# A four-layer graph network: long two-operand VectorE operations split or given a PSUM operand, and one small step of the last pass moved to GpSimd

## The chip, the cores and the metric

The kernel runs on one core of one Trainium2 chip. The metric is the device time of that core in microseconds, the median of the runs shown. Everything is float32 except the indices, which are int32.

## The reference

`x` is [50000, 256]; `src` and `dst` are 25000 edges sorted by `dst`. Four graph layers follow each other, each as `x = layernorm(x + layer(x))`:

```python
# layer 0: edges carry a product, nodes run an MLP with batch statistics
agg = segment_sum(x[dst] * edge_attr_256, src, N)
h1  = ((1 + eps) * x + agg) @ W1 + b1
out = relu(batchnorm(h1) * gamma + beta) @ W2 + b2
# layer 1: MLP over [x, mean of edge_attr_64 by src, u[0]]
out = relu(concat(x, agg64, u) @ W1 + b1) @ W2 + b2
# layer 2: attention over the edges of each dst, 8 heads of 32
e   = leaky_relu(a1[src] + a2[dst]); m = segment_max(e, dst)
ex  = exp(e - m[dst]); s = segment_sum(ex, dst)
out = elu(segment_sum(ft[src] * ex / s[dst], dst))
# layer 3: the same with 4 heads of 64, self loops, and out = elu(out + bias) + x
```

## The kernel before, in words

The program is seven stages, with a barrier of all engines after each (`barrier`). The rows of `x` go in steps of 512 (4 rows to each of 128 partitions, `J = 4`); that is 98 steps over the nodes (`NS`) and 49 over the edges (`ES`, `CS`). Each engine runs its own program in order; the order is written out by hand and kept by semaphore waits (`wait`, `wait_ge`). SyncE (SP) issues the large transfers, GpSimd (POOL) the indirect ones, one instruction for each 128 rows.

- **Stage 1** (`p1_*`), edges of layers 0 and 1. Before the steps SP fills a table `tab0` with zeros. POOL gathers `x[dst]` (L397, four per step) and scatter-adds the sums (L408, four per step). VectorE compares the step's source indices (L440), counts earlier equal ones with a masked reduction against the constant `early` (L446) and multiplies the gathered rows by `edge_attr_256` (L456, 1024 columns). TensorE adds rows of one source, ScalarE copies them out.
- **Stage 2** (`p2_*`) and **stage 3** (`p3_*`) are layer 0's batch statistics and the two MLPs. The change does not touch them.
- **Stage 4** is `edge_pass(2)`. POOL gathers the source rows of step s+3 (L1068) and scatters the finished rows of step s-1 (L1079), alternately, four of each per step. TensorE transposes and projects them; VectorE runs the running sum along each partition's edges: the products with the new weights (L1252), four times a multiply and an add of 256 columns (L1263, L1267), and a division over all 1024 columns (L1276). The scatters of a step wait for that one division.
- **Stage 5** is `node_pass`, elu, residual, layer norm and the projection for layer 3. ScalarE makes relu and exp (L1413, L1415), VectorE the elu (L1484) and the residual (L1487), both 1024 columns with two SBUF operands, statistics (L1493, L1497), the normalisation's shift (L1478) and the copy-out of the projection (L1471). ScalarE normalises (L1423) once the shift is there, and only behind that does it make the exp of the step after next. POOL computes the power (L1448) and scatters four narrow pieces per step (L1454).
- **Stage 6** is `edge_pass(3)`. It has no matmuls in its steps; L1256 multiplies 1024 gathered columns, then L1263 and L1267 run as in stage 4, and each scatter waits for its L1267.
- **Stage 7** is `last_pass`. POOL multiplies two blocks of 1024 columns (L1647, twice per step, back to back), adds the epsilon (L1653) and takes the power (L1656). TensorE adds the two blocks in PSUM (L1598), ScalarE makes relu and exp and the normalisation (L1624), VectorE the elu (L1712), the residual (L1716), `shift` (L1704: minus mean times the power's result, 4 columns, issued after L1716 of the next step), statistics (L1722, L1726) and, in even and odd steps, `factors` or `shares` (L1676 to L1697, 32 or 64 columns). SP loads three blocks and stores one per step, 2.1 MB together.

## Time and profile before

| | us |
|---|---|
| median of 3 runs | 5930.69 |
| the runs | 5925.17 to 5933.20 |
| the profiled execution, its own time | 5937.27 |
| the profiled execution, its span | 5935.2 |

The profile is of one execution; spans of single instructions come from it. "Idle before" names what ended an engine's idle time in front of a group. The busy share of the transfer engines ("DMA share") and the rate in GB/s stand in the view of the stretches. Engines are named PE (TensorE), PEld (its weight loads), DVE (VectorE), ACT (ScalarE), POOL (GpSimd) and SP (SyncE).

### The profile page before, as it was taken

To read this page: it belongs to the slowest core of one execution; us is meant where nothing else is said; L and a number is where in the kernel's file an instruction comes from. 1 tells how busy PE (TensorE), PEld (TensorE's weight loads), DVE (VectorE), ACT (ScalarE), POOL (GpSimd) and SP (SyncE) were. 2 spreads that over 40 slices of the span, in tenths; PEclk is the share of its full clock that TensorE was granted. 3 is DMA by queue.
4 is the path that set the end of the run, shared out by engine and by line. 5 is a ranking of instruction groups with operands and counts; after the bars stand their busy time and mean duration, and the time that the engine had idled before them with its cause. 6 is when DMAs were issued, how large, how long until landed. Compare 5 with 4: busy or idle time off the path is not lost. (4 is left out here: it accounts for less than half of the span.)

```text
span 5935.2 us, 70230 instructions
## 1 busy us (share of the span) xinstructions
PE 4263.1 (72%) x16758; PEld 2808.8 (47%) x16758; DVE 3817.1 (64%) x9802; ACT 1982.9 (33%) x3296; POOL 3712.2 (63%) x3263
## 2 busy tenths in 40 slices
PE   0566639989999999999999877756777500036665
PEld 0344415546666666666666567655555300012222
DVE  1344435656666666666666567767887655569998
ACT  0111105542222222222222222226777400026666
POOL 2378854445555555555555577766888777767776
PEclk6778869999999999999999988879999855568888
DMA  9987769983333333333333244438999633369997
GB/s 358 380 175 138 140 112 363 366 297 122 120 117 117 117 117 117 117 117 117 117 117 117 72 140 134 132 106 292 308 306 304 211 93 91 92 209 331 320 322 265
DMA packets 497940, 1125.24 MB, mean 190 GB/s; under 512 B 165814, under 2 KB 248714, under 8 KB 497814
## 3 DMA queue, kind: packets, MB, share of 16 engines
q1 hardware_dynamic: 346380, 913.22, 45.0%
q0 software_dynamic: 113184, 174.84, 12.4%
q10 hardware_dynamic: 38250, 35.85, 2.0%
q8 instruction: 36, 0.59, 0.0%
q14 instruction: 90, 0.74, 0.0%
HBM read 623.20 MB, written 543.83 MB: 197 GB/s over the span
## 5 line engine op out<-in xcount | busy, mean ns | idle before, releaser
L942 PE MATMUL psum<-arena,W1b 128*128 128x512 f32 x1568 | 725.3, 605 | 0.0
L965 PE MATMUL psum<-W2b,arena 128*128 128x256 f32 x3136 | 725.2, 379 | 0.0
L730 DVE TENSOR_SCALAR arena<-arena 128x256 f32<-128x256 f32 x784 | 462.4, 651 | 302.2 <-POOL arena L725 300.0
L536 PE MATMUL psum<-arena 128*128 128x324 f32 x980 | 362.9, 538 | 372.6 <-DVE arena L456 254.1
L1598 PE MATMUL psum<-arena,ident 128*128 128x512 f32 x784 | 433.5, 706 | 240.9 <-POOL arena L1647 240.9
L965 PEld LDWEIGHTS psum<-W2b,arena 128*128 128x128 f32 x3136 | 573.1, 190 | 66.3 <-issue 0.5
L855 ACT ACTIVATE arena<-psum,hbias 128x512 f32<-128x512 f32 x392 | 269.3, 687 | 860.2 <-PE psum L942 860.2
L1404 PE MATMUL psum<-Wg,arena 128*128 128x264 f32 x1568 | 396.6, 409 | 175.5 <-ACT arena L1429 175.5
L1454 POOL DMA_INDIRECT ad_d<-arena,FE x392 | 450.9, 1150 | 113.0 <-issue 111.2
L1079 POOL DMA_INDIRECT tab<-arena,IDX x392 | 412.7, 1053 | 122.9 <-issue 93.4
L721 POOL TENSOR_TENSOR arena<-arena,lneps 128x4 f32<-128x4 f32 x196 | 39.1, 200 | 713.9 <-DVE arena L717 711.3
L942 PEld LDWEIGHTS psum<-arena,W1b 128*128 128x128 f32 x1568 | 281.7, 189 | 429.9 <-issue 429.9
L819 POOL DMA_INDIRECT xd_d<-arena,FE x392 | 412.0, 1051 | 106.2 <-issue 105.9
L536 PEld LDWEIGHTS psum<-arena 128*128 128x128 f32 x980 | 229.8, 240 | 490.0 <-issue 379.5
L1404 PEld LDWEIGHTS psum<-Wg,arena 128*128 128x128 f32 x1568 | 304.5, 199 | 250.2 <-ACT arena L1429 198.8
L408 POOL DMA_INDIRECT tab<-arena x196 | 325.6, 1661 | 144.7 <-issue 54.6
L1598 PEld LDWEIGHTS psum<-arena,ident 128*128 128x128 f32 x784 | 168.2, 225 | 505.5 <-issue 482.8
L1138 PE MATMUL psum<-ident,arena 128*128 128x128 f32 x24 | 5.8, 433 | 543.9 <-DVE arena L1293 532.3
L1647 POOL TENSOR_TENSOR arena<-arena 128x1024 f32<-128x1024 f32 x196 | 368.9, 1903 | 18.0 <-DVE arena L1697 18.0
L918 PE MATMUL psum<-W2a,arena 128*128 128x256 f32 x1568 | 356.1, 380 | 23.0 <-ACT arena L841 23.0
L683 PE MATMUL psum<-arena,W1a 128*128 128x512 f32 x784 | 353.9, 594 | 0.0
L633 POOL DMA_INDIRECT fe_d<-EID,FIRST x196 | 200.0, 1021 | 242.9 <-ACT arena L658 198.3
(220 smaller groups left out, 9283.2 us busy)
## 6 DMA issues: line engine op xcount, KB each, us to landing
arena<-tab SPq DMA_DIRECT2D x194, 544.0 KB
arena<-in_x SPq DMA_DIRECT2D x194, 512.0 KB, 4.5
x_d<-arena SPq DMA_DIRECT2D x194, 512.0 KB, 3.6
arena<-x_d SPq DMA_DIRECT2D x194, 512.0 KB, 7.1
tab<-zero SPq DMA_DIRECT2D x132, 486.0 KB, 11.7
tab<-blank SPq DMA_DIRECT2D x97, 544.0 KB
h_d<-arena SPq DMA_DIRECT2D x97, 528.0 KB, 4.9
arena<-h_d SPq DMA_DIRECT2D x97, 528.0 KB, 5.6
```

Source lines behind the costliest of these rows:

```text
L536: last = pe.matmul(psum[:, 2 + j, 0:TW0], same[:, k.slot(2), i, j * P:(j + 1) * P], msg[:, k.slot(NX), i, :], start=(i == j), stop=(i == J ...
L683: last = pe.matmul(psum[:, 4 + 2 * b + g, :], W1a[:, f, g * P:(g + 1) * P], hT[:, b, f, :], start=(f == 0), stop=(f == FH - 1))
L730: v.tensor_scalar(y[:, j, :], r[:, j, :], self.mv[:, j, 0:1], self.rs[:, j:j + 1], ALU.subtract, ALU.mult).then_inc(self.s["y"], 1)
L819: pool.indirect_dma_start(out=xd_d[:, :], out_offset=bass.IndirectOffsetOnAxis(ap=FE[:, s * J + j:s * J + j + 1], axis=0), in_=x2[:, s % 2 ...
L918: last = pe.matmul(outA(j), p3y[:, f, j * P:(j + 1) * P], W2a[:, f, :], start=(f == 0), stop=(f == FH - 1))
L942: last = pe.matmul(psum[:, BR + c % RING, :], W1b[:, f, c * P:(c + 1) * P], x1T[:, f, :], start=False, stop=(f == FH - 1))
L965: last = pe.matmul(outB(j), hid[:, c, j * P:(j + 1) * P], W2b[:, c, :], start=(c == 0), stop=(c == KH - 1))
L1079: pool.indirect_dma_start(out=tab[:, :], out_offset=bass.IndirectOffsetOnAxis(ap=IDX[:, 2, c:c + 1], axis=0), in_=fin[:, s % NG, j, :], in ...
L1404: last = pe.matmul(psum[:, 2 + j, 0:HW], xT[:, f, j * P:(j + 1) * P], Wg[3][:, f, :], start=(f == 0), stop=(f == FH - 1))
L1454: pool.indirect_dma_start(out=ad_d[:, :], out_offset=bass.IndirectOffsetOnAxis(ap=FE[:, c:c + 1], axis=0), in_=hs[:, k.slot(NB), j, D + H3 ...
L1598: last = pe.matmul(psum[:, b + i, :], ident[:, :], a[:, k.slot(2), 2 * i:2 * i + 2, :].rearrange("p j d -> p (j d)"), start=(n == 0), stop ...
L1647: pool.tensor_tensor(out=a[:, b, :, :].rearrange("p j (h c) -> p j h c", h=H), in0=t[:, k.slot(NB), :, 0:D].rearrange("p j (h c) -> p j h ...
```

## The change

It touches five stages.

- Stage 1: `early` is copied once to PSUM bank 6, and the masked reduction reads it there. L456 becomes four multiplies of 256 columns. `hbias`'s matmuls move from bank 6 to bank 2.
- Stage 4: the maximum and the reciprocal of the sums are made before the running sum instead of behind it; L1276 becomes four divisions of 256 columns (`divided`), the one for row j issued after the add of row j+1; each scatter waits for its own division. The wait for the old scatter of the row buffer stands ahead of the running sum.
- Stage 5: the elu is written to PSUM in two operations of 512 columns; the residual reads it from there.
- Stage 6: the weights of a step are also written to PSUM, by a second exp on ScalarE (`near`), and the products of L1256 (`tB`) lie in PSUM; L1256, L1263 and L1267 then have one SBUF operand each.
- Stage 7: `shift` is gone from VectorE. VectorE makes minus the mean (`neg`, 4 columns) behind the step's statistics, after a wait for them, and GpSimd multiplies it by the power's result.

```diff
 # stage 1, VectorE
+            v.tensor_copy(psum[:, 6, :], early[:, :]).then_inc(s_c["id"], 1)
...
-                    v.tensor_tensor_reduce(out=junk[j], in0=same[:, b, j, 0:(j + 1) * P], in1=early[:, (J - 1 - j) * P:J * P], scale=1.0, scalar=0.0,
+                    v.tensor_tensor_reduce(out=junk[j], in0=same[:, b, j, 0:(j + 1) * P], in1=psum[:, 6, (J - 1 - j) * P:J * P], scale=1.0, scalar=0.0,
...
-                v.tensor_tensor(out=msg[:, k.slot(NX), :, 0:D], in0=xg[:, k.slot(NX), :, :], in1=eat[:, k.slot(NX), :, :], op=ALU.mult).then_inc(q["msg"], 1)
+                for j in range(J):
+                    v.tensor_tensor(out=msg[:, k.slot(NX), j, 0:D], in0=xg[:, k.slot(NX), j, :], in1=eat[:, k.slot(NX), j, :], op=ALU.mult).then_inc(q["msg"], 1)
 # stages 4 and 6, GpSimd's scatter
                     if L == 3:
                         pool.wait_ge(r["S"], J * s + j + 1)
-                    elif j == 0:
-                        pool.wait_ge(r["full"], s + 1)
+                    else:
+                        pool.wait_ge(r["full"], J * s + j + 1)
 # stages 4 and 6, ScalarE and VectorE
+                    if L == 3:
+                        act.activation(near(s), dd, ACT.Exp).then_inc(r["near"], 1)
...
+            tB = take([J, D]) if L == 2 else psum[:, 0:2, :].rearrange("p a (j d) -> p (a j) d", d=D)
...
+                    w1p, w2p = (w1[:, :, 1:J + 1], w2[:, :, 1:J + 1]) if L == 2 else (near(s)[:, 0, :, :], near(s)[:, 1, :, :])
...
+                    if L == 2:
+                        v.wait_ge(r["s"], s + 1)
+                        wait(v, r["full"], J * s)
+                        v.tensor_scalar(inv, sums[:, :, cur], 1e-30, None, ALU.max).then_inc(r["inv"], 1)
+                        v.wait_ge(r["inv"], 2 * s + 1)
+                        v.reciprocal(inv, inv).then_inc(r["inv"], 1)
+                    wait(v, sc[c], 16 * J * (s // NG))
...
+                        if L == 2 and j > 0:
+                            divided(s, j - 1)
+                    if L == 2:
+                        divided(s, J - 1)
+                def divided(s, j):
+                    if j == 0:
+                        v.wait_ge(r["inv"], 2 * s + 2)
+                    v.wait_ge(r["S"], J * s + j + 1)
+                    v.tensor_tensor(out=fin[:, s % NG, j, 0:D].rearrange("p (h c) -> p h c", h=H), in0=row[:, s % NG, j, 0:D].rearrange("p (h c) -> p h c", h=H),
+                                    in1=heads(inv[:, :, j]), op=ALU.mult).then_inc(r["full"], 1)
 # stage 5, VectorE
+                    for i in range(2):
+                        v.scalar_tensor_tensor(out=unit[:, 2 * i:2 * i + 2, :], in0=ex[:, b, 2 * i:2 * i + 2, :], scalar=-1.0,
+                                               in1=tt[:, k.slot(NB), 2 * i:2 * i + 2, 0:D], op0=ALU.add, op1=ALU.max).then_inc(r["elu"], 1)
...
-                    v.tensor_tensor(out=rr[:, b, :, :], in0=xt[:, k.slot(NB), :, :], in1=rr[:, b, :, :], op=ALU.add).then_inc(r["r"], 1)
+                    v.tensor_tensor(out=rr[:, b, :, :], in0=xt[:, k.slot(NB), :, :], in1=unit, op=ALU.add).then_inc(r["r"], 1)
 # stage 7, GpSimd's rstd, then VectorE
+                    pool.wait_ge(r["rs"], k.s + Z + 1)
+                    pool.wait_ge(r["neg"], k.s + 1)
+                    pool.tensor_tensor(out=nm[:, b, :], in0=neg[:, b, :], in1=rsd[:, b, :], op=ALU.mult).then_inc(r["nm"], 1)
...
-                    if not (k.known() and k.s == 0):
-                        shift(k.plus(-1))
...
+                    v.wait_ge(r["mv"], J * (k.s + Z + 1))
+                    wait(v, r["nm"], k.s + Z - 1)
+                    v.tensor_scalar(neg[:, b, :], mv[:, b, :, 0], -1.0, None, ALU.mult).then_inc(r["neg"], 1)
```

## Rows read from the trace of the kernel before

**Rows 1.** The page: span and instructions.

```profile
span 5935.2 us, 70230 instructions
```

**Rows 2.** Stretches of stages 4, 5, 6, 7: length, busy (instructions) by engine, clock, DMA share, GB/s.

```profile
3411.00:3994.00 583.00, 419.69 (x2408) 377.82 (x2408) 410.42 (x1346) 140.48 (x297) 430.69 (x395) 0.84 0.40 126
3996.00:4712.00 716.00, 501.07 (x2352) 390.27 (x2352) 556.58 (x1372) 496.81 (x784) 552.74 (x489) 0.95 0.91 294
4716.00:5253.00 537.00, 6.74 (x28) 5.99 (x28) 303.83 (x1049) 25.30 (x101) 404.74 (x394) 0.50 0.30 91
5256.00:5935.00 679.00, 433.52 (x784) 168.21 (x784) 601.29 (x1617) 408.37 (x637) 484.28 (x392) 0.86 0.90 309
```

**Rows 3.** GpSimd's transfer lines: ns (minimum/median/maximum), first and last start.

```profile
L397 POOL DMA_INDIRECT arena<-in_x,arena x196: 942/947/1850, 12.0 to 781.5; - x196
L408 POOL DMA_INDIRECT tab<-arena x196: 1552/1578/2385, 230.6 to 859.5; - x196
...
L1068 POOL DMA_INDIRECT arena<-x_d,IDX x196: 941/976/1934, 3417.6 to 3948.4; - x196
```

**Rows 4.** Groups by shape over the whole span: busy us, mean ns, idle before.

```profile
L408 POOL DMA_INDIRECT tab<-arena x196 | 325.6, 1661 | 144.7 <-issue 54.6 <-DMA tab<-zero 52.8 <-DMA tab<-arena 21.7
...
L397 POOL DMA_INDIRECT arena<-in_x,arena x196 | 195.8, 999 | 189.3 <-DVE arena L456 123.9 <-issue 52.1 <-DMA arena<-in_dst 6.2
```

**Rows 5.** Groups by shape inside stage 4, 3435 to 3985 us.

```profile
L1079 POOL DMA_INDIRECT tab<-arena,IDX x196 | 214.5, 1094 | 63.2 <-issue 61.1 <-PE psum L1113 1.5 <-ACT arena L1166 0.3
L1068 POOL DMA_INDIRECT arena<-x_d,IDX x184 | 201.4, 1095 | 64.9 <-issue 46.9 <-ACT arena L1156 12.9 <-ACT arena L1166 2.9
```

**Rows 6.** Timeline of one step of stage 4: start us, duration us.

```profile
3703.55 1.22 DVE L1276 TENSOR_TENSOR arena<-arena 128x1024 f32<-128x1024 f32 x1
3703.76 1.86 POOL L1068 DMA_INDIRECT arena<-x_d,IDX  x1 [0.30 <-issue]
```

**Rows 7.** Groups by shape inside stage 6, 4760 to 5230 us.

```profile
L1068 POOL DMA_INDIRECT arena<-h_d,IDX x176 | 184.3, 1047 | 53.7 <-issue 53.7
L1079 POOL DMA_INDIRECT tab<-arena,IDX x177 | 178.3, 1007 | 53.9 <-issue 28.3 <-DVE arena L1267 25.6
```

**Rows 8.** Timeline of one step of stage 5, DVE and ACT.

```profile
4301.34 1.23 DVE L1484 SCALAR_TENSOR_TENSOR arena<-arena 128x1024 f32<-128x1024 f32 x1 [0.78 <-ACT arena L1415]
...
4304.11 2.07 ACT L1423 ACTIVATE arena<-arena 128x256 f32<-128x256 f32 x4 [1.83 <-DVE arena L1478]
...
4308.26 1.23 DVE L1484 SCALAR_TENSOR_TENSOR arena<-arena 128x1024 f32<-128x1024 f32 x1 [0.60 <-ACT arena L1415]
```

**Rows 9.** Timeline of stage 4: two half-width operations with a PSUM operand, merged.

```profile
3709.72 1.26 DVE L1252 TENSOR_TENSOR arena<-psum,arena 128x512 f32<-128x512 f32 x2
```

**Rows 10.** VectorE lines of stages 7 and 3: minimum/median/maximum ns, first and last start.

```profile
L1712 DVE SCALAR_TENSOR_TENSOR psum<-arena,psum x98: 1205/1222/1230, 5281.4 to 5922.8; 128x1024 f32<-128x1024 f32 x98
L873 DVE TENSOR_SCALAR arena<-arena x98: 153/155/1905, 1325.9 to 3347.6; 128x4 f32<-128x4 f32 x98
```

**Rows 11.** Groups by shape inside stage 7, 5281 to 5923 us.

```profile
L1704 DVE SCALAR_TENSOR_TENSOR arena<-arena 128x4 f32<-128x4 f32 x96 | 113.7, 1185 | 0.0
...
L1653 POOL TENSOR_TENSOR arena<-arena,lneps 128x4 f32<-128x4 f32 x97 | 19.3, 199 | 151.8 <-DVE arena L1726 151.1
```

**Rows 12.** Timeline of one step of stage 7 in which L1704 did not wait.

```profile
5404.28 1.22 DVE L1712 SCALAR_TENSOR_TENSOR psum<-arena,psum 128x1024 f32<-128x1024 f32 x1
...
5404.89 3.77 POOL L1647 TENSOR_TENSOR arena<-arena 128x1024 f32<-128x1024 f32 x2
...
5409.84 1.23 DVE L1712 SCALAR_TENSOR_TENSOR psum<-arena,psum 128x1024 f32<-128x1024 f32 x1 [0.17 <-issue]
5410.01 3.77 POOL L1647 TENSOR_TENSOR arena<-arena 128x1024 f32<-128x1024 f32 x2
```

**Rows 13.** Transfers of stage 7 from 5300 to 5900 us.

```profile
DMA packets 51768, 192.82 MB, mean 321 GB/s; under 512 B 5764, under 2 KB 5764, under 8 KB 51767
```

**Rows 14.** Transfers of stage 2 from 900 to 1300 us.

```profile
DMA packets 79576, 142.71 MB, mean 357 GB/s; under 512 B 10349, under 2 KB 56250, under 8 KB 79569
```

70 lines of the change are left out of this document (30 added, 40 removed).

## The prediction

> **What bounds the kernel now.** I read the stretches first [rows 2], because a busy share over the whole span mixes stages with different limits. Then, for each stage that the change touches, I asked which engine never waits. The reader should see four answers.
>
> *Stages 1, 4 and 6* are held by GpSimd's queue of indirect transfers. In stage 4, 380 of them take 415.9 us busy [rows 5], and behind nearly each stands 0.30 us that waits for nothing the trace shows [rows 6], 114 us: 530 of that window's 550. In stage 6 it is 362.6 us busy and 353 times 0.30, 469 of 470 [rows 7]. In stage 1, from the first scatter at 230.6 us to the last at 859.5 [rows 3], the scatters take 325.6 us, the 168 gathers in that time 168 us, and the gaps 109 us: 603 of 629 [rows 4]. VectorE is busy for only 410 of 583 us and 304 of 537 [rows 2], so its own length is not the price there. What costs is how long GpSimd's instruction takes: a gather has a median of 0.976 us and a maximum of 1.934 [rows 3], and the long one starts 0.21 us into the 1024-column L1276 and takes 1.86 us [rows 6]. It does its 0.9 us of work after L1276 has ended.
>
> *Stage 5* looks the same but isn't. ScalarE waits 1.83 us per step for VectorE's shift; from the elu's start to that wait's end are 2.77 us, from there to the next elu's start 4.15 us, and the step is the sum, 6.92 us [rows 8]. It is a ring of ScalarE and VectorE; GpSimd runs beside it.
>
> *Stage 7* is held by VectorE: 98 starts of L1712 from 5281.4 to 5922.8 us are 6.61 us apart [rows 10], GpSimd waits 151 us for the statistics, and the shift on four columns takes 1.185 us on average [rows 11]. A 4-column operation needs 0.155 us when nothing is in its way [rows 10]; the rest is waiting while L1647 runs. In a step in which it didn't wait, L1712 to L1712 is 5.56 us, and GpSimd's period is 5.12 [rows 12]. Transfers run at 90% busy [rows 2].
>
> **The change, part by part.** The sum is made against the profiled execution, 5937.3 us (span 5935.2 [rows 1]); the median shown, 5930.7, is 6.6 lower, and I carry the difference over to it.
>
> *Stage 1.* Gathers average 0.999 us against a median of 0.947, scatters 1.661 against 1.578 [rows 3, 4]: 196 times 0.052 and 0.083 is 26 us over the median, the most that can be got. The masked reduction no longer has two SBUF operands; the multiply still has, in pieces that can hold GpSimd a third as long. I take two thirds, **-18 us**; the ends are -26 and 0. The split costs VectorE three more fixed parts, about 0.155 each, what an operation on 4 columns takes [rows 10], 0.5 us a step, hidden under the queue. The copy to PSUM and the moved bank cost nothing: the fill of the table covers them until 230 us.
>
> *Stage 4.* The excess is 196 times (1.095 - 0.976) for gathers and 196 times (1.094 - 1.007) for scatters, the base of the latter from stage 6's mean: 40 us [rows 3, 5, 7]. One L1276 per step takes 0.88 us of it [rows 6] when it meets a start; 49 would be 43. The divisions in quarters stay two-SBUF operations of the kind of L1267, and stage 6, full of those, has 0.07 us excess on gathers and none on scatters [rows 3, 7]. I take **-25 us**; ends -40 and 0. VectorE gets the same 0.5 us a step longer, and has 3.5 idle [rows 2]. The earlier wait for the old scatter concerns one issued before the gathers this step waited for. VectorE's step would be some 9.0 us, under the queue's 10.8 (530 us over 49). Next late would be ScalarE's copy, already 12.9 us [rows 5].
>
> *Stage 5.* Blocked scatters get shorter, but lie beside the ring: 0. On the ring the elu becomes two halves. Two 512-column operations with a PSUM operand take 1.26 us together [rows 9] against 1.23 [rows 8]; I add one wait's slack and take 0.05 us for 98 steps, **+5 us**. Ends: 0, and 0.2 a step, +20.
>
> *Stage 6.* The three products leave the two-SBUF kind altogether. Gathers average 1.047 against 0.976; 196 times 0.07 is 14, **-13 us**, ends -14 and 0. The second exp of ScalarE (a few tenths of a us) and its wait stand where VectorE has 4.7 us idle per step [rows 2]; were that cover gone, 49 times 0.3 would be 15 us.
>
> *Stage 7.* VectorE loses the shift, 1.185 us a step, and gains the negation, 0.155 [rows 10], and the wait for the statistics, about 0.1 (no row shows it; between 0 and 0.2): 6.61 - 1.185 + 0.255 is 5.68 us. GpSimd gains an operation of L1653's size, 0.2 us [rows 11], and its wait, 0.14: 5.12 + 0.34 is 5.46 [rows 12]. Behind this wait stand L1647's two products, but both sides of it start from the same statistics, so it ends early. Then transfers are next: 192.8 MB in 600 us is 2.13 MB a step of 6.61 us [rows 10, 13]; at stage 2's 357 GB/s [rows 14] that takes 5.97. The three lie so close that the slowest plus a little jitter holds: 6.0 us. 97 times (6.61 - 6.0) is **-59 us**. Ends: 5.7 a step, -88; 6.35, -25.
>
> The rows on which the negation hangs: L873, also a scalar operation on 4 columns, takes 0.155 us by median and once 1.905 [rows 10], so it can be held too. The Trainium skill, "SBUF — State Buffer", section Who interferes with whom, says that a `tensor_scalar` in a two-port mode and a GpSimd instruction fully block each other; the trace agrees, and by that alone the negation would be no better placed than the shift. I don't take it so, because GpSimd is idle, waiting for these very statistics, when they end: 151 us of waiting in 97 steps [rows 11].
>
> Sum: -18 - 25 + 5 - 13 - 59 = -110 us. 5930.7 - 110 is **5821 us**.
>
> **The rivals.** *The transfer queues aren't eased (12%).* The long gathers would come from something else than the two-SBUF kind. For it: no row shows what a long transfer of stage 1 lies beside. Against it: [rows 6]. Then stages 1, 4 and 6 give 0, 5931 - 54 = 5877. A rule of the Trainium skill, same page and section, points that way: it infers that `tensor_tensor` does not stall descriptor generation, which needs the write interface. The row with 1.86 us speaks against it.
>
> *Transfers hold stage 7 near today's rate (13%).* They are 90% busy already; 6.35 us a step gives -25 there and 5855 in all.
>
> *Stage 7 runs at VectorE's 5.7 us (6%).* 5792.
>
> *The negation waits like the shift did (6%).* Then stage 7 is 6.61 + 0.1 a step, +10; 5931 - 51 + 10 = 5890.
>
> *Slower (3%).* The two L1647 stand back to back for 3.77 us [rows 12]. If the negation fell behind both in every step, VectorE's step would be 5.5 + 3.77 = 9.3 us, stage 7 +260, the whole 6140. It decides from a mean wait of 1.5 us on: then the step is 7.14, which eats the 51 us of the other stages. Against it: GpSimd idle at that point.
>
> **How the numbers follow.** The forecast has 60%. The range 5785 to 5882 takes in the forecast with its bounds and the first three rivals, and leaves out the last two and the far ends. A measurement of this kernel tells about 0.2%, 12 us, from no change. All cases but the last are faster by more; I leave 3% for same because several small terms could fall out together: 0.94, 0.03, 0.03.
>
> **What would show it.** Stage 4: no transfer of GpSimd near 1.9 us, means near 1.02; the stage some 558 us. Stage 6: gathers all near 0.98, the stage 524. Stage 5: the step 6.92 to 7.0, scatters shorter, GpSimd waiting more. Stage 7: L1712 about 6.0 us apart, transfers at 350 GB/s, the negation at 0.15 to 0.3 us. I am wrong if the negation averages over 1 us, if the 0.30 us gaps grow, or if stage 5 moves by more than 20 us.

## The result, and the profile after

The changed kernel takes **5887.75 us** (median of 4 runs, 5881.5 to 5894.84) against 5931.67 for the kernel before (4 runs): a ratio of 0.9925, 95% interval 0.9913 to 0.9937. The forecast was 5821 us with a range of 5785 to 5882, so it was faster, as said, but by 44 us in place of 110, and the time lies above the range. The ratios of this document leave out two executions far outside the rest (8714 us in run e13, 8141 in run e15).

The page of the changed kernel, its span:

```profile
span 5892.9 us, 71391 instructions
```

Its stretches of stages 4, 5, 6 and 7, with columns as in [rows 2]:

```profile
3397.00:3963.00 566.00, 421.52 (x2408) 379.08 (x2408) 406.52 (x1493) 140.43 (x297) 411.19 (x395) 0.83 0.41 130
3965.00:4695.00 730.00, 512.93 (x2352) 400.06 (x2352) 562.87 (x1470) 497.81 (x784) 502.52 (x490) 0.93 0.89 288
4697.00:5222.00 525.00, 6.73 (x28) 5.98 (x28) 300.84 (x1049) 29.67 (x150) 391.30 (x395) 0.50 0.31 93
5224.00:5892.00 668.00, 419.40 (x784) 164.56 (x784) 550.61 (x1617) 403.63 (x637) 505.20 (x490) 0.87 0.90 314
```

Windows are cut by hand and a few us off. For sums I use the time from GpSimd's drain at one stage's end to the next, in the profiled execution of each kernel. That is one execution of each; the changed kernel's is the slowest of its four (5894.84 us), so that single terms are good to some us and no better:

```
stage (us)         1      2       3      4      5      6      7
kernel before    863.3  447.1  2100.1  584.6  718.7  541.1  673.1
changed kernel   848.4  447.2  2100.2  568.3  732.1  526.6  663.8
difference       -14.9   +0.1    +0.1  -16.3  +13.4  -14.5   -9.3
forecast           -18      -       -    -25     +5    -13    -59
```

Two terms come within some 3 us of the forecast, two miss it by 8 or 9. The fifth, stage 7, is short by 50.

The groups of GpSimd's transfers in stages 1, 4 and 6 of the changed kernel (us busy, mean ns, idle before), which answer to [rows 4, 5, 7]. L409, L398, L1088 and L1077 are the L408, L397, L1079 and L1068 of before:

```profile
L409 POOL DMA_INDIRECT tab<-arena x195 | 311.5, 1597 | 95.4 <-issue 54.3 <-DMA tab<-arena 22.3 <-DVE arena L456 18.3
L398 POOL DMA_INDIRECT arena<-in_x,arena x164 | 159.8, 974 | 50.0 <-issue 42.7 <-DVE arena L456 6.7 <-ACT arena L358 0.6
...
L1088 POOL DMA_INDIRECT tab<-arena,IDX x196 | 208.4, 1063 | 63.3 <-issue 53.0 <-ACT arena L1165 4.3 <-DVE arena L1298 2.4
L1077 POOL DMA_INDIRECT arena<-x_d,IDX x196 | 200.0, 1021 | 69.1 <-issue 43.0 <-ACT arena L1165 16.2 <-ACT arena L1177 6.2
...
L1088 POOL DMA_INDIRECT tab<-arena,IDX x196 | 197.2, 1006 | 59.7 <-issue 37.5 <-DVE arena L1287 22.2
L1077 POOL DMA_INDIRECT arena<-h_d,IDX x196 | 191.1, 975 | 59.8 <-issue 58.6 <-DVE arena L1287 0.9 <-ACT arena L1177 0.3
```

The first pair is stage 1, the second stage 4, the third stage 6. In stage 6 the gathers went from 1047 to 975 ns. In stage 4 both kinds are shorter, but not at the 976 and 1007 ns that I took for unhindered. Counted over stage 4, 33 transfers took over 1.5 us before and none does now.

Groups of stage 7 (VectorE and GpSimd) of the changed kernel. L1735 and L1739 are the elu and the residual (before L1712 and L1716), L1750 is the new negation, L1704 to L1712 are `factors`, and L1678 is before's L1653 [rows 11]:

```profile
L1735 DVE SCALAR_TENSOR_TENSOR psum<-arena,psum 128x1024 f32<-128x1024 f32 x98 | 120.0, 1224 | 24.7 <-ACT arena L1642 21.9 <-issue 2.5
L1739 DVE SCALAR_TENSOR_TENSOR arena<-arena,psum 128x1024 f32<-128x1024 f32 x98 | 119.6, 1221 | 23.3 <-ACT arena L1649 15.5 <-DVE psum L1735 6.3
...
L1706 DVE SCALAR_TENSOR_TENSOR arena<-arena 128x32 f32<-128x32 f32 x49 | 22.9, 468 | 1.7
L1708 DVE TENSOR_TENSOR arena<-arena 128x32 f32<-128x32 f32 x49 | 20.9, 427 | 1.7
...
L1750 DVE TENSOR_SCALAR arena<-arena 128x4 f32<-128x4 f32 x98 | 16.6, 170 | 3.4
L1711 DVE TENSOR_TENSOR arena<-arena 128x32 f32<-128x32 f32 x49 | 14.5, 295 | 1.7
L1704 DVE TENSOR_TENSOR arena<-arena 128x32 f32<-128x32 f32 x49 | 14.4, 293 | 39.1 <-DMA arena<-tab 36.1 <-issue 2.6
L1712 DVE TENSOR_TENSOR arena<-arena 128x32 f32<-128x32 f32 x49 | 12.5, 255 | 0.0
...
L1678 POOL TENSOR_TENSOR arena<-arena,lneps 128x4 f32<-128x4 f32 x98 | 19.7, 201 | 118.5 <-DVE arena L1747 115.1
```

The negation takes 170 ns: the part of the forecast that concerned the moved step came true, and the 1.0 us for which the shift was held each step is gone. Three things stand in its place. The five lines of `factors` sum to 85.2 us, where in the run with GpSimd's wait below the same five take 50.3. VectorE waits 36 us for table rows, 19 of them before the stage's first step, as in every run. And it waits 21.9 and 15.5 us for ScalarE. The kernel before had the second in small: its first line of `factors` waited 23.5 us, the same 19 at the start and 4 later.

```profile
L1676 DVE TENSOR_TENSOR arena<-arena 128x32 f32<-128x32 f32 x49 | 10.1, 206 | 23.6 <-DMA arena<-tab 23.5
```

The first two can be seen in one step of the changed kernel's timeline (start us, duration us):

```profile
5409.51 0.17 DVE L1750 TENSOR_SCALAR arena<-arena 128x4 f32<-128x4 f32 x1
...
5411.20 0.19 DVE L1704 TENSOR_TENSOR arena<-arena 128x32 f32<-128x32 f32 x1 [1.53 <-DMA arena<-tab]
5411.25 3.77 POOL L1672 TENSOR_TENSOR arena<-arena 128x1024 f32<-128x1024 f32 x2
5411.43 1.78 DVE L1706 SCALAR_TENSOR_TENSOR arena<-arena 128x32 f32<-128x32 f32 x1
5413.24 1.83 DVE L1708 TENSOR_TENSOR arena<-arena 128x32 f32<-128x32 f32 x1
5415.10 0.19 DVE L1711 TENSOR_TENSOR arena<-arena 128x32 f32<-128x32 f32 x1
...
5415.31 1.22 DVE L1735 SCALAR_TENSOR_TENSOR psum<-arena,psum 128x1024 f32<-128x1024 f32 x1
```

The table row of the step lands 1.5 us late, so `factors` starts together with GpSimd's two products (L1672), and two operations on 32 columns wait for one whole product each. From L1735 at 5404.84 to this one the step takes 10.5 us. The ten longest steps of the stage all have this form: a wait of 0.9 to 1.5 us for the table, then two operations of 1.8 to 1.9 us. Of the 97 steps 40 are under 5.8 us, as forecast for VectorE alone, and 10 are over 8.5; the mean is 6.51. Before it was 6.61 with 59 steps between 6.2 and 7. The loss is no longer spread evenly. It sits in a few long steps.

### The profile page after: what moved, and what is told of

It reads as the page before. It is cut to its first block and busy times, and to the rows that moved or that the text cites. A ratio compares the mean times of both kernels' runs of the same rounds, so it can differ in the third digit from the quotient of the medians.

```text
span 5892.9 us, 71391 instructions
## 1 busy us (share of the span) xinstructions
PE 4264.3 (72%) x16758; PEld 2816.8 (48%) x16758; DVE 3772.7 (64%) x10195; ACT 1984.3 (34%) x3345; POOL 3632.6 (62%) x3361
## 5 line engine op out<-in xcount | busy, mean ns | idle before, releaser
L1623 PE MATMUL psum<-arena,ident 128*128 128x512 f32 x784 | 419.4, 687 | 243.9 <-POOL arena L1672 235.8
L1426 PE MATMUL psum<-Wg,arena 128*128 128x264 f32 x1568 | 409.9, 419 | 169.9 <-ACT arena L1451 169.9
L1088 POOL DMA_INDIRECT tab<-arena,IDX x392 | 405.6, 1035 | 123.1 <-issue 90.5
L1476 POOL DMA_INDIRECT ad_d<-arena,FE x392 | 400.7, 1022 | 113.3 <-issue 113.0
L409 POOL DMA_INDIRECT tab<-arena x196 | 313.1, 1597 | 147.3 <-issue 54.3
L1672 POOL TENSOR_TENSOR arena<-arena 128x1024 f32<-128x1024 f32 x196 | 369.3, 1906 | 18.0 <-DVE arena L1725 15.5
```

What stands on the lines that cost most here:

```text
L1088: pool.indirect_dma_start(out=tab[:, :], out_offset=bass.IndirectOffsetOnAxis(ap=IDX[:, 2, c:c + 1], axis=0), in_=fin[:, s % NG, j, :], in ...
L1426: last = pe.matmul(psum[:, 2 + j, 0:HW], xT[:, f, j * P:(j + 1) * P], Wg[3][:, f, :], start=(f == 0), stop=(f == FH - 1))
L1476: pool.indirect_dma_start(out=ad_d[:, :], out_offset=bass.IndirectOffsetOnAxis(ap=FE[:, c:c + 1], axis=0), in_=hs[:, k.slot(NB), j, D + H3 ...
L1623: last = pe.matmul(psum[:, b + i, :], ident[:, :], a[:, k.slot(2), 2 * i:2 * i + 2, :].rearrange("p j d -> p (j d)"), start=(n == 0), stop ...
L1672: pool.tensor_tensor(out=a[:, b, :, :].rearrange("p j (h c) -> p j h c", h=H), in0=t[:, k.slot(NB), :, 0:D].rearrange("p j (h c) -> p j h ...
```

## The experiments

All but the runs whose edit says otherwise start from the changed kernel. The runs fell on five chips. On those of the first four and the last three runs the kernel before takes 5936 and 5938 us. On the other three chips (eleven runs) it takes 6027, 6034 and 6029 us, and so much of the difference lies in stages 4 and 6 that every run there has to be read stage by stage. Each chip was used at one time only, so "chip" below may also stand for something else that differed between those times. Durations as above:

```
stage (us)                        1      4      5      6      7
first four runs
e1  stage 5 as before           848.5  566.2  718.3  526.2  653.8
e2  GpSimd's wait               848.4  567.3  732.3  526.2  644.2
e3  six table slots             848.8  566.0  730.9  526.3  659.0
e4  fewer bytes                 850.0  566.7  731.0  526.3  618.0
other chips
e5  e1 + e2                     848.6  631.8  718.0  599.3  643.0
e6  e1 + e2 + e3                850.6  634.0  719.2  593.8  626.1
e7  only stage 7 changed        860.2  630.7  718.3  582.4  665.5
e8  three splits undone         859.9  630.7  723.5  591.7  678.6
e9  e2 + e4                     849.4  643.2  732.7  602.2  614.9
e10 before, fewer bytes         862.1  643.6  717.5  583.9  664.7
e11 division whole              847.5  637.9  730.6  599.5  657.0
e12 as e6                       848.7  640.5  721.0  596.9  623.2
e13 changed kernel              851.1  633.2  732.5  600.6  661.9
e14 as e11                      851.6  633.3  732.8  598.4  657.8
e15 as e6                       849.7  631.4  719.0  595.2  627.5
last three runs
e16 empty waits in stage 6      851.5  568.2  732.2  526.4  658.0
e17 stage 6 as before           850.7  565.9  730.9  541.3  665.6
e18 e6 with fewer waits         851.4  563.0  718.5  526.2  660.5
```

The changed kernel's own stage 7 spreads from 654 to 666 us over the profiles in which it is unaltered (e8 has 679). So less than some 12 us in stage 7 of one profile says nothing, and e8 shows that even 25 can occur.

### Stage 5 as it was

```diff
-                    for i in range(2):
-                        v.scalar_tensor_tensor(out=unit[:, 2 * i:2 * i + 2, :], ...)
+                    v.scalar_tensor_tensor(out=rr[:, b, :, :], in0=ex[:, b, :, :], ...)
...
-                    v.tensor_tensor(out=rr[:, b, :, :], in0=xt[:, k.slot(NB), :, :], in1=unit, ...)
+                    v.tensor_tensor(out=rr[:, b, :, :], in0=xt[:, k.slot(NB), :, :], in1=rr[:, b, :, :], ...)
```

> The changed kernel with stage 5 as it was before. Stage 5 took 13.5 us more after the change (732.2 against 718.7 us between the drains) while its scatters got shorter. Theory: GpSimd was beside the ring of ScalarE and VectorE, so undoing the edit gives the 13 us back: about 5874 us. Rival: the stages disturb each other, and the loss stays: 5887.

Ratio 0.9913 (0.9895 to 0.9931), and stage 5 is back at 718.3 us: its edit costs 13.8. By median the whole is only 7 us shorter (5880.87), within what stage 7 varies; the run doesn't decide between 5874 and 5887 for the whole, but stage 5 itself came back, here and at 718.0 in e5. Groups of VectorE in stage 5, first the changed kernel, then this run:

```profile
L1506 DVE SCALAR_TENSOR_TENSOR psum<-arena 128x512 f32<-128x512 f32 x196 | 127.4, 695 | 78.7 <-ACT arena L1437 78.7
L1493 DVE TENSOR_TENSOR arena<-psum,bias 128x1056 f32<-128x1056 f32 x98 | 123.3, 1258 | 64.4 <-PE psum L1426 62.4 <-issue 0.3
L1511 DVE TENSOR_TENSOR arena<-arena,psum 128x1024 f32<-128x1024 f32 x98 | 119.6, 1221 | 11.2 <-DVE psum L1506 9.4
```

```profile
L1493 DVE TENSOR_TENSOR arena<-psum,bias 128x1056 f32<-128x1056 f32 x98 | 123.3, 1258 | 56.7 <-PE psum L1426 56.6
L1509 DVE TENSOR_TENSOR arena<-arena 128x1024 f32<-128x1024 f32 x98 | 120.1, 1225 | 7.6
L1506 DVE SCALAR_TENSOR_TENSOR arena<-arena 128x1024 f32<-128x1024 f32 x98 | 120.0, 1224 | 79.7 <-ACT arena L1437 79.7
```

The halves hold VectorE 7.4 us longer (127.4 against 120.0), the residual waits 3.6 more, and the copy-out of the projection 7.7 more for TensorE, whose granted clock is 0.93 in place of 0.95. That is 18.7 us of the ring, somewhat more than the stage lost. Whether the clock is a cause of the longer wait for TensorE or goes along with the longer step isn't shown.

### GpSimd waits for the factors

```diff
                     rstd(k)
+                    if k.slot(2) == 0 and live(k.plus(4), NS):
+                        pool.wait_ge(r["d"], 2 * (k.plus(4).turn(2) + 1))
                     if live(k.plus(3), NS):
                         shared(k.plus(3))
```

> The changed kernel, in stage 7 GpSimd's products of an even step wait until VectorE has made that step's factors. Theory A (late table, then blocked factors): 12 of the 97 steps take 10.2 to 10.5 us, because the factors start late, behind a transfer, and two of their small operations then each wait for a whole 1.9 us product. With the guard these steps take 7 to 8 us, and the kernel 25 to 35 us less, about 5857. Rival B (the transfers' rate holds the stage): the waits only move, same time within 8 us. Rival C (GpSimd is the bound): GpSimd now waits longer, 10 to 20 us slower.

Ratio 0.989 (0.9873 to 0.9907). Stage 7 takes 644.2 us, 19.6 less, and no step is over 8.5 us. The whole is 17 us shorter by median, less than the 25 to 35 that I expected. In e5 the stage comes out at 643.0 again. Its groups of VectorE:

```profile
L1708 DVE SCALAR_TENSOR_TENSOR arena<-arena 128x32 f32<-128x32 f32 x49 | 11.2, 228 | 1.7
L1706 DVE TENSOR_TENSOR arena<-arena 128x32 f32<-128x32 f32 x49 | 11.0, 224 | 65.7 <-DMA arena<-tab 64.4 <-issue 1.2
```

The factors are no longer held, but VectorE now waits 64 us for the table rows in place of 36 (46 in place of 17 behind the first step). Part of what the wait saves goes into this.

### Six slots for the table rows

```diff
-            tt = take([NB, J, TW])
-            ht = take([NB, J, HW])
+            NQ, PER = 6, 12
+            tt = take([NQ, J, TW])
+            ht = take([NQ, J, HW])
...
-                    if live(k.plus(NB + 3), NS):
-                        tables(k.plus(NB + 3))
+                    if live(k.plus(NB + 5), NS):
+                        tables(k.plus(NB + 5))
```

> The changed kernel, in stage 7 the blocks of the table and of h have six slots instead of four and are loaded two steps earlier. Theory A: the factors never wait for a transfer, so they don't fall behind the products; the steps of 10 us go, stage 7 from 664 to 605-620 us, the kernel about 5835. Rival B (the rate of the transfers holds the stage): the queue is only longer, stage 7 stays within 15 us of 664. Rival D (TensorE at its lower clock and ScalarE hold it): the long steps go, but the others stay at 6.3 on average, stage 7 about 640.

Ratio 0.9904 (0.9887 to 0.992), stage 7 at 659 us. VectorE's groups:

```profile
L1739 DVE SCALAR_TENSOR_TENSOR psum<-arena,psum 128x1024 f32<-128x1024 f32 x98 | 120.1, 1225 | 66.5 <-ACT arena L1646 41.7 <-issue 24.6
...
L1708 DVE TENSOR_TENSOR arena<-arena 128x32 f32<-128x32 f32 x49 | 11.2, 229 | 23.2 <-DMA arena<-tab 18.6 <-issue 2.9
```

The wait for the table rows is gone but for the first two (18.6 us in all), and so is the holding of `factors`; the elu (here L1739) idles 66.5 us instead, 24.6 of them with no releaser. That last part isn't a wait of the schedule. Five steps take 11.6 to 12.2 us, and each is the first behind a jump of VectorE's loop: `run_beats` writes `PER` steps into the loop's body, 12 here in place of 4, and the five are steps 24, 36, 48, 60 and 72, counted from 0. One such step, VectorE alone, and below it the same place in e15, which also has six slots:

```profile
5395.44 0.23 DVE L1729 TENSOR_TENSOR arena<-arena 128x64 f32<-128x64 f32 x1
5401.71 1.23 DVE L1739 SCALAR_TENSOR_TENSOR psum<-arena,psum 128x1024 f32<-128x1024 f32 x1 [6.05 <-issue]
```

```profile
5516.34 0.23 DVE L1729 TENSOR_TENSOR arena<-arena 128x64 f32<-128x64 f32 x1
5516.87 1.23 DVE L1739 SCALAR_TENSOR_TENSOR psum<-arena,psum 128x1024 f32<-128x1024 f32 x1 [0.30 <-issue]
```

The trace has the branch itself in e3 at 5395.54 us and VectorE's next instruction, a register operation of the loop, at 5401.60. The five jumps of e3 take 5.7 to 6.4 us. In every other run but e18 no jump of VectorE takes over 0.28 us, in any stage. Counted from when the elu had all it waits for, the five cost 27 us. Without them stage 7 would be near 632 us (an estimate, 659 less 27), close to the 626 of e6: the six slots by themselves bring some 30 us, and the slow jumps take them back here. By its total this run looked like the rival in which the transfers' rate holds the stage, and it isn't: e6, e12 and e15 move the same bytes at 332 to 335 GB/s, against 314 in the changed kernel (e12's stretch of stage 7):

```profile
5356.00:5982.00 626.00, 417.77 (x784) 162.83 (x784) 516.59 (x1617) 403.11 (x637) 504.22 (x490) 0.88 0.94 335
```

### Fewer bytes in stage 7

The x rows are loaded for 16 of 128 partitions from the fifth step on, so part of the final sum is computed from old rows.

```diff
+                    if not (k.known() and k.s < NB):
+                        a, n = a[0:16], 16
                     sp.dma_start(xt[0:n, b, :, :], a).then_inc(n_x[b], 16)
```

> The changed kernel, in stage 7 the rows of x come from HBM for 16 of the 128 partitions only, from the fifth step on (what is computed from the other rows is not the reference's). A quarter of the stage's bytes is gone, nothing else. Theory A: tables land in time, stage 7 600 to 620 us. Rival B: the rate was the bound, stage 7 falls by up to a quarter until VectorE's 5.6 us a step holds, 560 to 580. Rival D: 640 or more.

Stage 7 falls to 618 us, 46 less, in the stretch

```profile
5224.00:5844.00 620.00, 408.17 (x784) 159.03 (x784) 516.93 (x1617) 404.08 (x637) 504.78 (x490) 0.90 0.83 269
```

The transfer engines are busy 0.83 of the time in place of 0.90, and TensorE is granted 0.90 in place of 0.87. The five lines of `factors` take 50.2 us, and behind the first step VectorE waits 2 us for table rows in place of 17. Two further runs say what these 46 us are. The first has this cut and GpSimd's wait together:

> The changed kernel with both: stage 7 reads x rows for 16 of 128 partitions from its fifth step on (part of the sum is left out), and GpSimd waits for the factors. The question is whether late transfers and blocked factors are one loss or two. One chain (a late table row makes the factors start behind the product): with few bytes the table is hardly late, the wait has nothing to save, stage 7 stays near the 618 us that fewer bytes alone gave, within 5. Two losses: 618 - 20 = 598 us.

614.9 us, 3 less than the cut alone: **one chain**. The held factors are a consequence of the late table rows, as the timeline above shows for one step, and as the six slots show with all bytes moved: there too both go together. The second makes the same cut in the kernel before:

> The kernel before with the same cut of stage 7's x rows. If the kernel before was bound by VectorE and its blocked shift, as I read it, transfers were hidden and stage 7 stays within 10 us of its 673, at 663 or more. Rival: the transfers held the stage before as well, and most of the 46 us that the same cut saved in the changed kernel are saved here too: 630 or less. In that case the change's small gain in stage 7 is what the transfers left of it.

664.7 us, 8 below 673: there VectorE and its held shift did set the pace and hid the transfers. So my reading of the kernel before was right, and what stood next was wrong: removing the shift uncovered the late table rows at once.

### Putting the parts together, and taking one alone

First the edits of e1 and e2 together, then those of e1, e2 and e3, then the kernel before with `last_pass` taken whole from the changed one. Their diffs are those shown.

> The first two runs together: stage 5 as in the kernel before, and GpSimd's wait for the factors in stage 7. The theory is that the two costs have nothing to do with each other, so the gains add up: stage 5 near 718 us, stage 7 near 644, the whole 5888 - 13.5 - 20 = 5854 us, ratio about 0.987 to the kernel before. Rival: the run with stage 5 undone was only 7 us below the changed kernel by median though its stage 5 was 14 shorter, because stage 7 varies from run to run by several us; then the sum of two such changes can come out anywhere from 5850 to 5870, and stage 7 would be over 650.

Stage 5 at 718.0, stage 7 at 643.0 us: the two gains add up. The whole, 5995.55 us, shows the other chip: ratio 0.9945 (0.9928 to 0.9961).

> As the last one, with six slots for the table rows instead of four. Theory that the late table rows and the blocked factors are one chain (table late, factors start behind the product): with the wait in place the late table costs only its own delay, and the extra slots take that away too; stage 7 about 635 us, the whole 5845. Rival: transfers run at the rate that the stage can get, so buffers move no time; stage 7 stays at 644 and the whole at 5854.

Stage 7 at 626.1 us, 17 less than with the wait alone, more than I gave it (and 623.2 and 627.5 in e12 and e15); ratio 0.9923 (0.9907 to 0.994).

> The kernel before with the last pass of the changed one and nothing else. If the stages are independent, stages 1, 4, 5 and 6 have the durations of before (863, 585, 719, 541 us) and stage 7 has 664 (9 less than before): the whole 5931 - 9 = 5922, ratio 0.998. Rival: stage 7 of the changed kernel suffers from the state in which stage 6 leaves it, or from the elu's count; then it is here nearer to my forecast, about 615 us, and the whole 5873.

665.5 us in stage 7 and 718.3 in stage 5, as in the changed kernel and the kernel before: for these two the stages are independent, and stage 7's small gain is its own. Ratio 0.9983 (0.997 to 0.9996), as expected.

### The three splits undone

```diff
-                for j in range(J):
-                    v.tensor_tensor(out=msg[:, k.slot(NX), j, 0:D], ...)
+                v.tensor_tensor(out=msg[:, k.slot(NX), :, 0:D], ...)
...
-                        if L == 2 and j > 0:
-                            divided(s, j - 1)
-                    if L == 2:
-                        divided(s, J - 1)
+                    if L == 2:
+                        v.wait_ge(r["S"], J * (s + 1))
+                        v.tensor_tensor(out=fin[:, c, :, 0:D].rearrange("p j (h c) -> p j h c", h=H), ...).then_inc(r["full"], J)
...
-                    for i in range(2):
-                        v.scalar_tensor_tensor(out=unit[:, 2 * i:2 * i + 2, :], ...)
+                    v.scalar_tensor_tensor(out=unit, in0=ex[:, b, :, :], ...)
```

The elu still goes to PSUM.

> The changed kernel with each operation whole again that was split by column: stage 1's multiply (both operands in SBUF), stage 4's division (both in SBUF) and stage 5's elu, which still writes PSUM. Stage 7 unchanged. Theory that a long operation with two SBUF operands holds GpSimd's queue and its pieces do so a third as long: stage 1 goes back by over half of its 15 us (to 857 or more, with gathers of 1.8 us again), stage 4 goes back by 16 (to 584, with transfers near 1.9 us). Rival: the gain came from the PSUM operand of the masked reduction in stage 1, which stays at 849; in stage 4 only the division's split could bring it. Stage 5: if the second half's fixed part is the cost, the ring is 0.07 us a step shorter and the stage loses 7 of its 13.5 us (725); if the cost comes from something else, the stage stays at 732.

Stage 1 goes to 859.9 us. On this chip the stage as before takes 860.2 (e7) and the changed one 848.6 and 850.6 (e5, e6), so the whole of the gain there comes from cutting the multiply, whose operands both stay in SBUF. The scatters show it, the gathers don't:

```profile
L409 POOL DMA_INDIRECT tab<-arena x196 | 325.4, 1660 | 163.8 <-DMA tab<-zero 70.2 <-issue 54.8 <-DMA tab<-arena 22.5
L398 POOL DMA_INDIRECT arena<-in_x,arena x164 | 159.6, 973 | 50.0 <-issue 44.5 <-DVE arena L456 4.9 <-ACT arena L358 0.6
```

The scatter is at 1660 ns again as before the change [rows 4], while the gather keeps its 973: that part comes from the masked reduction's operand in PSUM, and it is worth 0.3 us of the stage here, less than stage 1 varies (847.5 to 851.6 in the runs that leave it as changed). Stage 5 takes 723.5 us: 8.6 of its 13.4 are the split, the other 5 the PSUM operand or the TensorE clock that goes with it, which this run doesn't separate. Stage 4 couldn't be judged by its length on this chip (630.7, as the old edit has there too).

### Stage 4's division whole

The second of these three edits alone, on two chips.

> The changed kernel with stage 4's division whole again, one operation of 1024 columns with two SBUF operands in place of four of 256. Theory: each long gather or scatter of the kernel before came from this one operation; stage 4 goes from 568 back to about 584 us where stage 4 isn't held by something else, and transfers near 1.9 us are there again, 30 or more. Rival: the stage gained from the earlier release of the scatters, a quarter at a time; then the transfers near 1.9 us return but their mean hardly moves and half of the 16 us stays.

> As for the earlier run of the same edit. On a chip like the first ones stage 4 takes 584 us in place of 568 if one operation of 1024 columns with two SBUF operands is what blocked GpSimd; the mean of gathers and scatters there rises from 1.02 and 1.04 to 1.04 and 1.09. On a chip like the later ones stage 4 stays where the changed kernel's is, within 6 us, and only the means move. Rival as before: half of the gain stays.

Both fell on chips of the longer kind. There stage 4 is as long as the changed kernel's (637.9 beside 640.5 and 643.2; 633.3 beside 633.2). The transfers over 1.5 us come back, 19 and 12 of them where the changed kernel has none (30 or more were expected), and GpSimd's busy time in stage 4 rises by 6 us on the second chip (413.5 against 407.5). That the one division caused the long transfers is shown. That it is worth 16 us of stage 4 on the first chips is argued, not shown: there GpSimd's busy time fell by 19.5 us (430.69 [rows 2] to 411.19) and the stage by 16.3, which fits, but the rival, the earlier release of the scatters, was never run on such a chip.

### The change on the other chips

The changed kernel with no edit at all:

> The changed kernel as it is. On a chip like the first ones: stages 4, 5, 6, 7 in 568, 732, 526, 664 us, ratio 0.9925. On a chip like those of the last two jobs (kernel before at 6027 to 6034): stages 4 and 6 at 632 and 597, no shorter or even longer than the kernel before's 631 and 583 there, so that the gain is that of stages 1 and 7 less the loss of stage 5: ratio 0.998 to 1.001. Rival: the 30 us of stages 4 and 6 come on top there too, and the ratio is 0.993.

Ratio **1.0005** (0.9995 to 1.0015): on this chip the change gives nothing. Its stretches of stages 4 and 6:

```profile
3398.00:4030.00 632.00, 474.61 (x2408) 414.88 (x2408) 409.58 (x1493) 136.92 (x297) 407.51 (x395) 0.76 0.37 116
4763.00:5362.00 599.00, 6.73 (x28) 5.98 (x28) 305.80 (x1049) 29.68 (x150) 390.91 (x395) 0.50 0.27 81
```

GpSimd is busy as long as on the first chip (391 us in stage 6), but the stage is 74 us longer. VectorE's timeline has stretches like this one in stage 6:

```profile
4816.32 0.20 DVE L1216 TENSOR_TENSOR_SCAN arena<-KEEP,arena 128x20 f32<-128x20 f32 x1 [2.71 <-remote]
4819.82 0.18 DVE L1248 TENSOR_TENSOR arena<-arena 128x16 f32<-128x16 f32 x1 [3.30 <-remote]
4820.52 0.17 DVE L1250 SCALAR_TENSOR_TENSOR arena<-arena 128x16 f32<-128x16 f32 x1 [0.52 <-DVE arena L1248]
...
4828.34 0.20 DVE L1216 TENSOR_TENSOR_SCAN arena<-KEEP,arena 128x20 f32<-128x20 f32 x1
4828.57 0.18 DVE L1248 TENSOR_TENSOR arena<-arena 128x16 f32<-128x16 f32 x1
4828.78 0.17 DVE L1250 SCALAR_TENSOR_TENSOR arena<-arena 128x16 f32<-128x16 f32 x1
```

The first three rows are slow, the last three are the same operations a step later. They start within 0.44 us in the second case and within 4.2 in the first. L1216 waits for counts of VectorE's own copies alone, which had ended 2.7 us before; "remote" means that the trace has no instruction that released it. Over stage 6 two steps of some 20 and 18 us follow three of 6.6 to 9, in a pattern that returns every 5 steps; with the old edit (e7, e10) it returns every 5 or 6. The stages that do this are the two in which VectorE's steps are written out one by one (`for s in range(S0, S1)`), where it loops in the others (`run_beats`); these have the same durations on all chips, within the spread of stage 7. Written-out steps alone aren't enough: GpSimd's are written out in stages 1 and 5 too. That the loading of instructions is behind it fits this and the slow jumps of e3 and e18, and is not shown for either. Stage 6 with the new edit takes 592 to 602 us on these chips and 582 and 584 with the old one: there the stage is about 15 us longer with the edit, where on the first chips it is 14.5 shorter. The two with the old edit have the old stages 4 and 5 in front of them too, so that this isn't shown to be the edit's own. Three runs were to test the count of instructions. e16 adds empty waits,

```diff
+                    if L == 3:
+                        for _ in range(8):
+                            v.wait_ge(r["B"], 2 * CS + g)
```

> The changed kernel with eight more waits on VectorE in each step of stage 6, each on a count that was reached a step before, so that they stop nothing. Theory for chips on which the kernel before takes 6027 us or more: in the stages whose steps are written out the late starts come with the number of instructions passed (29.5 recorded for VectorE in a step of the changed kernel, 28.5 before, and about 0.18 us lost for each: 600 us less 49 steps of 6.7 us, over 49 times 29.5). Eight more then cost 49 x 8 x 0.18 = 70 us: stage 6 at about 660 us there, with the late stretches every 4 steps in place of 5. Rival: the late starts come with time or with transfers, not with instructions; then stage 6 stays at 600 within 10. On a chip like the first ones: 526 us, VectorE's own 0.3 us a step being hidden.

e17 undoes stage 6's edit,

```diff
-            tB = take([J, D]) if L == 2 else psum[:, 0:2, :].rearrange("p a (j d) -> p (a j) d", d=D)
+            tB = take([J, D])
...
-                    if L == 3:
-                        act.activation(near(s), dd, ACT.Exp).then_inc(r["near"], 1)
```

> The changed kernel with the edit of stage 6 undone and nothing else. On a chip like the later ones: stage 6 goes from 600 back to 583 us, since the edit adds one instruction a step to VectorE and one to ScalarE. On a chip like the first: from 526 back to 541. Rival for the later chips: the 15 us that stage 6 was longer there come from where the stage begins in the instruction stream, not from its own edit; then it stays near 598.

and e18 is the combination e6 with repeated waits left out:

```diff
-                        v.wait_ge(r["B"], 2 * s + j // 2 + 1 if L == 2 else 2 * CS + g + 1)
+                        if j % 2 == 0 if L == 2 else j == 0:
+                            v.wait_ge(r["B"], 2 * s + j // 2 + 1 if L == 2 else 2 * CS + g + 1)
```

> The combination (stage 5 as before, GpSimd's wait for the factors, six table slots) with the repeated waits for the same product taken out: two a step in stage 4, three a step in stage 6. On a chip like the later ones, by the theory of 0.18 us for each instruction: stage 4 631 - 18 = 613 at best (less where GpSimd's queue covers it), stage 6 595 - 26 = 569, the whole 5984 - 35 = 5949, ratio 0.987. Rival: late starts have nothing to do with the count; then 0.992 as before. On a chip like the first ones the ratio is 0.984, with or without these waits.

All three came to a chip of the first kind, so the theory stays untested. Eight empty waits cost nothing there (526.4 us), and stage 6 undone gives 541.3: the edit is worth 14.7 us by itself. Its gathers:

```profile
L1077 POOL DMA_INDIRECT arena<-h_d,IDX x196 | 205.0, 1046 | 59.8 <-issue 58.9 <-DVE arena L1282 0.6 <-ACT arena L1175 0.3
```

They are at 1046 ns again, the 1047 of [rows 7].

### The combination

> Stage 5 of the kernel before, GpSimd's wait for the factors and six table slots once more, beside the kernel before in more rounds: the last time it stood on a chip on which stages 4 and 6 of every kernel were 60 us longer and hid the gain of the change there. If this chip has the durations of the first ones (stage 4 of the changed kernel 568 us, stage 6 526), the whole is 5888 - 13.5 - 38 = 5836 us, ratio 0.984; if stages 4 and 6 are again 630 and 595, the ratio is 0.992 as before.

> Stage 5 as before, GpSimd's wait for the factors, six table slots. Against the changed kernel of this same job: stage 5 shorter by 13.5 us and stage 7 by 38 to 41, so 52 us below it by median whatever the chip, as those two stages had the same durations on each chip so far. Rival: on some chip stage 7 is held by the transfers alone and the slots give nothing: then 33 us below.

0.9917 (0.9903 to 0.993) and 0.9923 (0.9903 to 0.9943) on two chips of the longer kind; on the second it is 48 us below the changed kernel on the same chip (5983.91 against 6032.37), close to the 52 expected. With the repeated waits taken out it then ran on a chip of the first kind (e18): 0.989 (0.9874 to 0.9907), 5871.71 us, not the 0.984 that I expected there, and no better than GpSimd's wait alone. Stage 5 is at 718.5, but stage 7 at 660.5 in place of 626. Its stretch, and one long step of its timeline, ScalarE's exp for the elu first:

```profile
5206.00:5872.00 666.00, 424.92 (x784) 167.79 (x784) 516.56 (x1617) 403.04 (x637) 503.95 (x490) 0.84 0.90 315
```

```profile
5373.80 1.06 ACT L1645 ACTIVATE arena<-arena 128x1024 f32<-128x1024 f32 x1
...
5377.11 0.23 DVE L1730 TENSOR_TENSOR arena<-arena 128x64 f32<-128x64 f32 x1
...
5384.72 1.23 DVE L1740 SCALAR_TENSOR_TENSOR psum<-arena,psum 128x1024 f32<-128x1024 f32 x1 [7.38 <-issue]
```

The exp that this elu waits for ended at 5374.86 and VectorE's own last operation at 5377.34, so nothing in the schedule holds it for 7.38 us. It is the jump of the loop again: the branch stands at 5377.21 and the next instruction at 5384.61. The five jumps of this run take 6.0 to 7.3 us, those of e6, e12 and e15, also with 12 steps in the loop, 0.25 at most. VectorE idles 55.8 us before the elu in the 17 steps over 7 us, against 21.3 in the 10 of e15; from the elu's readiness on the five jumps cost 29 us, nearly all of the 33 between 660.5 and 627.5. Why the jumps are slow in e3 and e18 and not in the other three is open: the chips differ, and so does the code in front of the loop. The body is long in all five (337 to 349 recorded VectorE instructions in one round, against 118 with 4 steps).

So the combination is the best of the versions tried on the chips of the longer kind, by 0.8% below the kernel before. On the first kind the nearest to it that ran (e18) and GpSimd's wait alone stand level at 0.989, both below the changed kernel's 0.9925; e18 gets there by stage 5, and its stage 7 is 16 us longer than with the wait alone (644.2). Stage 5 as before with the wait and four slots (e5) did not run on the first kind.

## Why the prediction was wrong

- **Stage 1**: -18 forecast, -14.9. Right in size. I had not said which of the two edits would bring it; undoing the cut of the multiply alone (e8) brings back 11 us, all that there was to win on that chip.
- **Stage 4**: -25, came -16.3. Right in kind: the long transfers are gone, and return with the division. The term was too large by 9 us. I took L1276 for nearly all of the excess over 976 and 1007 ns; after it had gone, 45 and 56 ns a transfer were left, some 20 us, where I had left 15. The other 4 us are not accounted for.
- **Stage 5**: +5, came +13.4. That GpSimd's shorter scatters are worth nothing was right: they went from 1150 to 1022 ns, and GpSimd's wait for VectorE grew in their place. The mis-sized term is the elu in halves. I priced it by two operations that read PSUM [rows 9], 1.26 us, and these, which write it, take 1.30; and I gave the wait in between next to nothing (it is 0.04 us longer in each of 98 steps) and the copy-out's wait for TensorE, 7.7 us longer now, no part.
- **Stage 6**: -13, came -14.5, -14.7 for the edit alone. Right. The Trainium skill, "SBUF — State Buffer", section Who interferes with whom, infers that `tensor_tensor` does not stall descriptor generation. These runs show that GpSimd's indirect transfer as a whole is stalled: each of the three lines here is a `tensor_tensor`, and gathers are at 1046 ns when they have two SBUF operands and at 975 when one is in PSUM. Which part of the instruction waits, the making of descriptors or the reading of its indices, no run here shows.
- **Stage 7**: -59, came -9.3, no more than the stage varies; this is the step that failed. The sentence was: "The three lie so close that the slowest plus a little jitter holds: 6.0 us." The runs measure two of the three paces, and these were about right: VectorE's clean steps take 5.5 to 5.9 us, and the transfers move all bytes at 6.09 to 6.14 us a step once there are six slots (e6, e12, e15). But I added them as if they were independent, and "a little jitter" stood in for a coupling: a table row that is late by 1.5 us moves `factors` into GpSimd's products, and there two 32-column operations cost 3.6 us in place of 0.4. The late rows and what hangs on them are 46 us (e4). I had named the very mechanism, for the negation alone, and asked of no other small operation on VectorE whether it would now start beside L1672. Before the change the same five lines took 58 us, so they were hardly held; now 85. The two small waits in the sum, 0.1 us for VectorE's statistics and 0.14 for GpSimd's, stood on no row; the runs show 0.03 and 0.10 (3.4 us before L1750 and 9.6 before GpSimd's new product, L1684, over 98), so that they didn't matter.
- **The rivals**: "Transfers hold stage 7 near today's rate (13%)" came nearest, in that the transfers are what the stage waits on. But it isn't their rate: it was 309 GB/s before and 314 after, and 332 to 335 with six slots. It is that rows come late for four slots. At 6.35 us a step the rival was still too hopeful; the mean is 6.51. Nor did VectorE's own 5.7 us (6%) hold, but for the 40 short steps. That the negation waits like the shift (6%) and the slower case (3%) did not occur: 170 ns. That the queues aren't eased (12%) fell with the means of stage 6.
- **The range** ended at 5882, 6 us too low. It took the other cases one at a time, and here stages 4 and 5 missed upwards together, by 17 us, on top of stage 7.

## What to carry to other kernels

When three engines stand within 10% of each other, the forecast for "remove the slowest" is not the next slowest: list every small operation of two SBUF operands and ask what it starts beside once the schedule shifts. A transfer that is late by 1.5 us then costs three times as much. Look also at idle time that nothing released: here it was the jump of a loop whose body an edit of the buffers had made three times as long, and by the total alone the edit seemed to give nothing. And measure on more than one chip before a gain under one per cent is believed: 0.75% on one kind was 0.0% on the other. GpSimd's wait for the factors held on both (stage 7 at 644 and 643 us), the six slots did not (660 and 626).

## What the runs showed of the hardware

- Small operations on VectorE with two SBUF operands (32 columns, 0.19 us by themselves) took 1.78 and 1.83 us when they started beside GpSimd's products of 1024 columns (1.9 us each), one operation for each of two products back to back.
- GpSimd's indirect transfers are held in the same way by a long VectorE operation with two SBUF operands (1.86 us in place of 0.98 beside one of 1024 columns). It was enough to move one operand of VectorE's operation to PSUM (stage 6: longest gather 0.985 us) or to cut it into quarters (stage 4: none over 1.3).
- The jump at the end of a VectorE loop, from the branch to the next instruction, took 5.7 to 7.3 us in stage 7 of e3 and e18, where the loop's body has 337 recorded instructions or more, and 0.28 us or less in all other stages and runs. Three of these (e6, e12, e15) have a body as long and 0.25 us at most.
- The chips differ: one and the same kernel takes 5931 to 5938 us by median on some and 6027 to 6034 on others, by what stages 4 and 6 take.
